# A two-stage attention and gated-mixing kernel: two more operand sets built on chip, the weights prepared in other gaps, and a re-ordered last row

## The chip, the cores and the metric

The kernel runs on one core of a Trainium2 chip. The metric is the device time of one execution in microseconds (us), lower is better. It was run three times: 956.33, 957.35 and 960.95 us, median 957.35.

## The reference

The input `x` is 4 batches x 1024 tokens x 128 channels, float32. Two residual stages follow each other:

```python
x = x + layernorm(attention(layernorm(x), weight))
x = x + layernorm(mixing(layernorm(x), W_r, W_k, W_v, mu_r, mu_k))

# attention: 16 heads of 8 channels; queries and keys are both y, values are all 128 channels
scores = einsum('bhtk,bhsk->bhts', y, y) / sqrt(8)
o = einsum('bhts,bsc->bhtc', softmax(scores), x)          # x here is the normalised input
out = o (all heads side by side, 16*128 wide) @ weight    # weight: 2048 x 128

# mixing: the token before is mixed in, then a gate and a squared relu
r = sigmoid((mu_r*x + (1-mu_r)*x_prev) @ W_r.T);  k = (mu_k*x + (1-mu_k)*x_prev) @ W_k.T
out = r * (relu(k)**2 @ W_v.T)
```

## The kernel before, in words

**Units of work.** The tokens are cut into 8 rows of 512 (two rows to a batch). A *step* j is one head of one row, so there are 8 x 16 = 128 steps, and each step is two *quads* k = 2j, 2j+1 of 4 blocks of 128 keys: 256 quads in all. The five engines have programs of their own, each an ordered list written by a loop `for k in range(LAST)`, and they meet only at semaphores. An instruction that waits holds back everything behind it on its engine.

**One quad.** `score(k)` on TensorE (line 573, four matmuls of 32 rows) makes 4 x 512 scores in PSUM `ps_s`; `weigh(k)` on ScalarE (line 753) takes their exponential to `e_f`, float32; `cast(k)` (line 424) is a DMA, issued by GpSimd, which writes `e_hi`, the float16 part; `split_quad(k)` on VectorE (line 1103) makes the rest, `e_lo`; `products(k)` on TensorE (lines 592 to 594, twelve matmuls) multiplies both with the split values into `ps_o`. The loop runs `products(k-4)` behind `score(k)` (LAG is 4). Quad 0 has no DMA: VectorE casts it (`round_first`).

**One step.** After its second quad ScalarE takes the result (`take_o`, line 763), VectorE takes its rest (`split_o`, 1109), TensorE multiplies by the head's weights (`project`, 607 to 609, twelve matmuls), VectorE inverts the denominators (`invert`, 1115), ScalarE scales (`scale`, 770) and VectorE adds (`add`, 1122 and 1125). `project(j)` waits until `scale(j-1)` has read `ps_r`; it stands at k = 8 + 2j.

**Score operands.** A score matmul reads `op_s` and `op_t`: for each head the 8 channels in a high part, a low part, and rows with constants and a bound. They are made by transposing the normalised input (`turn_y`, `turn_shift` on TensorE, `take_y`, `take_shift` on ScalarE), writing it to scratch memory in DRAM (`keep_hi`, `keep_lo`, `keep_shift` on the SP queue) and reading it back per head into a ring of four slots (`load_s`, `load_t`, 8 DMAs a step). Since that round trip is long, the operands of the first two steps (`FIRST = 2`, quads 0 to 3) are built on chip: `first_operands` on VectorE (lines 1055 to 1064, 11 instructions) and on TensorE (lines 529 and 538), with ScalarE moving them to the ring. Those of step 2 are loaded by ScalarE's queue (`load_first_t`, 758) and SP, the others by SP (lines 308 and 315).

**Weights.** `weights_less(i)`, i = 0 to 3, subtracts on TensorE a column from four heads' weights (line 552, float32); `weight_base(i)` on VectorE finishes it (1075, 1076); `square_weights`, `weight_sum`, `keep_weight_sum`, `weight_scale` find a scale; `weights_high`, `weights_low` and `weights_neg` make the float16 parts. All must be there before `project(0)`.

**The last row.** After the loop the last step and the second stage of the last row are run in two halves of 256 tokens: `last_take`, `last_split`, `last_project`, `last_invert`, `last_scale`, `last_add`, a norm, a second norm, `last_turn`, `last_zT`, `last_mix`, then `last_key`, `last_gate`, `last_kv` on TensorE, and on VectorE per half `last_gated`, `last_centre`, `last_root`, `last_grow`, each half with its own norm and store. Exponential, square root and tanh need table loads on ScalarE, which the program forces early with a one-element `idle` activation (lines 950, 957, 963).

The loops around the change, in the tensor engine's program:

```python
            first_operands()
            for k in range(LAST):
                if k == LAG - 1:
                    products(0)
                if k == LAG:
                    weights_less(1)
                    weights_less(2)
                    products(1)
                    weights_less(3)
                    weight_sum()
                if k in (LAG + 1, LAG + 2):
                    products(k - LAG + 1)
                if k < QUADS:
                    score(k)
```

Of the kernel before, what the change touches and what calls it, by code (L numbers as in the profile page):

```python
# [30 lines left out]
def sandwich(nc, x, weight, w_r, w_k, w_v, mu_r, mu_k, out):  # L31
# [18 lines left out]
    FIRST = 2  # L50

    ctx = ExitStack()
    with ctx:
# [51 lines left out]

        yf = sb("yf", [P, NB, FIRST * HS], F32)
        sqf = sb("sqf", [P, RB, FIRST * HS], F32)
        n2f = sb("n2f", [P, 2, RB * FIRST], F32)
        comb_s = sb("comb_s", [P, NB, FIRST, 4, HS], F16)
        comb_t = sb("comb_t", [P, RB, FIRST, 4, HS], F16)  # L110

# [130 lines left out]
        def weights_ps(i):  # L242
            return (ps_r[:], ps_r[:], ps_x[:], ps_r[:])[i]
# [25 lines left out]
        def _(sp):  # L269
# [31 lines left out]
            def load_s(j):  # L301
                slot = j % OP_RING
                ge(sp, scored, 2 * (j - OP_RING + 1))
                if j % (2 * H) == 0:
                    sp.wait_ge(scr_s_in[batch_of(j)], 3 * 16)
                    sp.wait_ge(scr_const, 16 * B)
# [3 lines left out]
            def load_t(j):  # L310
                slot = j % OP_RING
                if j % (2 * H) == 0:
                    sp.wait_ge(scr_t_in[batch_of(j)], 4 * 16)
# [6 lines left out]
            sp.wait_ge(scr_const, 16)  # L320
            sp.wait_ge(scr_s_in[0], 3 * 16)
            for j in range(FIRST, OP_RING):
                load_s(j)
            sp.wait_ge(scr_t_in[0], 4 * 16)
            for j in range(FIRST + 1, OP_RING):
                load_t(j)
            for k in range(LAST):
# [17 lines left out]
                if k % 2 == 0 and k // 2 + OP_RING < STEPS:  # L345
# [14 lines left out]
        def _(pool):  # L360
# [21 lines left out]
            nc.gpsimd.memset(comb_s[:, :, :, 3, :], 1.0 / HS).then_inc(comb_const, 1)  # L382
# [92 lines left out]
        def _(pe):  # L475
# [41 lines left out]
            def weight_sum():  # L517
                pe.wait_ge(w_squared, 1)
                pe.wait_ge(w_based, 3)
                nc.tensor.matmul(ps_x[:, 0:1], ones[:], w_sum[:, 0:1], start=True, stop=True).then_inc(w_total, 1)  # L520

            def first_operands():
                pe.wait_ge(comb_s_ok, 1)
                pe.wait_ge(comb_const, 1)
                for h in range(FIRST):
                    for g in range(4):
                        for q in range(2):
                            at = h * 2 * P + q * P
                            mm = nc.tensor.transpose(f16(ps_o[32 * g:32 * g + 32, 0, :])[:, at:at + P],
                                                     comb_s[:, 2 * g + q, h].rearrange("p i k -> p (i k)"), ident16[:])  # L530
                mm.then_inc(first_s, 1)
                pe.wait_ge(comb_t_ok, 1)
                for h in range(FIRST):
                    for i in range(RB):
                        for g in range(4):
                            here = slice(32 * g, 32 * g + 32)
                            dst = f16(ps_o[here, 1, :] if h == 0 else ps_r[here, :])
# [855 lines left out]
```

## Time and profile before

| | |
|---|---|
| runs | 956.33, 957.35, 960.95 us; median 957.35 |
| the profiled execution | 956.48 us, of which the span of its trace is 954.7 us (1.8 us lie around it) |
| TensorE matmul busy | 909.0 us, 95% of the span |
| VectorE / ScalarE / GpSimd busy | 851.3 (89%) / 753.1 (79%) / 329.8 us (35%) |
| mean granted clock of TensorE | 0.986 of full |
| chain that ended last | PE 79%, DVE 5%, POOL 5%, DMA 4% |

TensorE is busy nearly everywhere: of 40 slices only the first two and the last two are under nine tenths. Busy time of matmuls overlaps, so the distance between two starts is the better price of one. The engines are named PE (TensorE; PEld its weight loads), DVE (VectorE), ACT (ScalarE), POOL (GpSimd) and SP in the rows.

### The profile page before, as it was taken

Reading aid. Unit: us, or ns where it says so; the run is one execution under the profiler, and the core shown is the slowest. Engines: PE = TensorE matmul, PEld = TensorE weight load, DVE = VectorE, ACT = ScalarE, POOL = GpSimd, SP = SyncE. Lnnn points to the kernel's source line nnn. Section 1 sums busy time; section 2 is a strip of 40 time slices with the busy share of each in tenths; the row PEclk is TensorE's granted clock in tenths of the full one; section 3 lists DMA queues with packets and bytes.
Section 4 is the critical chain, followed back from the end, with each engine's and each line's share of the span. In section 5 each row is a group of like instructions: output and inputs, shape, how many; then the busy total and the mean of one; then the engine's idle time right before and its main releaser. Section 6 shows DMA issues by size and latency. Waiting matters only on the chain.

```text
span 954.7 us, 17710 instructions
## 1 busy us (share of the span) xinstructions
PE 909.0 (95%) x5979; PEld 439.7 (46%) x5979; DVE 851.3 (89%) x1111; ACT 753.1 (79%) x1047; POOL 329.8 (35%) x484
## 2 busy tenths in 40 slices
PE   4799999999999999999999999999999999999982
PEld 2244444444444444444444444545444444544442
DVE  6789899898899989998988989999889899988976
ACT  5777788888879778888778777888877887788854
POOL 2111413532134634525126262443114451162310
PEclk9999999999999999999999999999999999999995
DMA  5899999999999888999988988899988989889820
GB/s 162 180 213 200 199 199 210 207 202 207 181 182 187 177 179 174 210 193 214 184 180 175 198 167 174 178 220 206 198 178 179 193 180 189 175 174 197 175 56 23
DMA packets 99465, 173.50 MB, mean 182 GB/s; under 512 B 21296, under 2 KB 62128, under 8 KB 99376
## 3 DMA queue, kind: packets, MB, share of 16 engines
q0 software_dynamic: 36720, 133.71, 72.7%
q1 hardware_dynamic: 62464, 38.54, 14.6%
q8 instruction: 48, 0.79, 0.3%
q14 instruction: 41, 0.34, 0.1%
q10 hardware_dynamic: 192, 0.13, 0.1%
HBM read 28.12 MB, written 10.49 MB: 40 GB/s over the span
## 4 chain that ended last, share of the span: by engine, by line
PE 79%; DVE 5%; POOL 5%; DMA 4%; issue 4%; ACT 2%; ACTq 0%; DVEq 0%; POOLq 0%
PE ps_o L592 22%; PE ps_o L594 19%; PE ps_o L593 19%; PE ps_s L573 7%; DMA e_hi<-e_f 4%; PE ps_r L607 3%; PE ps_r L609 3%; PE ps_r L608 3%; DVE e_lo L1103 1%; ACT e_f L753 1%; POOL e_hi L424 1%; POOL fnw L396 1%; POOL nw L394 1%; PE ps_x L634 1%; PE ps_x L630 1%
## 5 line engine op out<-in xcount | busy, mean ns | idle before, releaser
L1103 DVE TENSOR_TENSOR e_lo<-e_f,e_hi 128x2048 f16<-128x2048 f32 x256 | 585.0, 2286 | 64.7 <-DMA e_hi<-e_f 64.3
L753 ACT ACTIVATE e_f<-ps_s 128x2048 f32<-128x2048 f32 x256 | 481.6, 1881 | 135.4 <-PE ps_s L573 128.5
L592 PE MATMUL ps_o<-e_hi,y_hi 128*128 128x512 f16 x1024 | 391.9, 383 | 5.4 <-DVE o_neg L1109 4.8
L594 PE MATMUL ps_o<-e_hi,y_lo 128*128 128x512 f16 x1024 | 389.3, 380 | 0.0
L593 PE MATMUL ps_o<-e_lo,y_hi 128*128 128x512 f16 x1024 | 389.3, 380 | 0.0
L424 POOL DMA_DIRECT2D e_hi<-e_f x255 | 141.5, 555 | 563.0 <-ACT e_f L753 473.6
L592 PEld LDWEIGHTS ps_o<-e_hi,y_hi 128*128 128x128 f16 x1024 | 99.8, 97 | 156.1 <-issue 56.9
L770 ACT ACTIVATE part<-ps_r,rden 128x128 f32<-128x128 f32 x508 | 144.7, 372 | 33.7 <-DVE rden L1115 33.4
L594 PEld LDWEIGHTS ps_o<-e_hi,y_lo 128*128 128x128 f16 x1024 | 100.4, 98 | 121.9 <-issue 1.6
L593 PEld LDWEIGHTS ps_o<-e_lo,y_hi 128*128 128x128 f16 x1024 | 100.5, 98 | 92.2 <-issue 1.8
L573 PE MATMUL ps_s<-op_t,op_s 32*128 32x512 f16 x1024 | 102.5, 388 | 7.0 <-ACT e_f L753 5.6
L607 PE MATMUL ps_r<-w_hi,o_hi 128*128 128x128 f16 x508 | 91.8, 219 | 0.0
L608 PE MATMUL ps_r<-w_lo,o_hi 128*128 128x128 f16 x508 | 91.8, 219 | 0.0
L609 PE MATMUL ps_r<-w_neg,o_neg 128*128 128x128 f16 x508 | 91.7, 219 | 0.0
L1125 DVE TENSOR_TENSOR acc<-acc,part 128x512 f32<-128x512 f32 x119 | 82.9, 697 | 9.0 <-ACT part L770 8.5
L1109 DVE SCALAR_TENSOR_TENSOR o_neg<-o_hi,ps_o 128x512 f16<-128x512 f16 x127 | 85.7, 675 | 0.8 <-ACT o_hi L763 0.8
L763 ACT ACTIVATE o_hi<-ps_o 128x512 f16<-128x512 f32 x127 | 76.2, 600 | 1.3 <-PE ps_o L594 1.3
L573 PEld LDWEIGHTS ps_s<-op_t,op_s 32*128 32x128 f16 x1024 | 26.4, 91 | 69.5 <-issue 50.9
L608 PEld LDWEIGHTS ps_r<-w_lo,o_hi 128*128 128x128 f16 x508 | 49.8, 98 | 15.0 <-issue 0.3
L607 PEld LDWEIGHTS ps_r<-w_hi,o_hi 128*128 128x128 f16 x508 | 49.8, 98 | 15.0 <-issue 0.3
L609 PEld LDWEIGHTS ps_r<-w_neg,o_neg 128*128 128x128 f16 x508 | 49.8, 98 | 0.0
L1115 DVE RECIPROCAL rden<-ps_r 128x4 f32<-128x4 f32 x127 | 22.1, 174 | 5.3 <-PE ps_r L609 4.9
(223 smaller groups left out, 501.2 us busy)
## 6 DMA issues: line engine op xcount, KB each, us to landing
e_hi<-e_f POOLq DMA_DIRECT2D x255, 512.0 KB, 4.9
op_t<-scr_t SPq DMA_DIRECT2D x500, 32.0 KB, 3.6
op_s<-scr_s SPq DMA_DIRECT2D x504, 16.0 KB, 3.5
scr_s<-yT SPq DMA_DIRECT2D x12, 256.0 KB, 4.8
scr_t<-yT SPq DMA_DIRECT2D x12, 256.0 KB, 5.3
out_dram<-res SPq DMA_DIRECT2D x7, 256.0 KB, 5.5
xs<-in_L_attn_x_dram SPq DMA_DIRECT2D x3, 512.0 KB, 6.5
scr_s<-eighth SPq DMA_DIRECT2D x4, 256.0 KB, 5.3
```

The costliest lines, as they stand in the source:

```text
L424: nc.gpsimd.dma_start(flat(e_hi[:, ring]), flat(e_f[:, k % EF_RING])).then_inc(cast_in[ring], 16)
L573: mm = nc.tensor.matmul(ps_s[:, g, :], op_s[here, slot, q * P:(q + 1) * P], op_t[here, slot, :], start=True, stop=True)
L592: nc.tensor.matmul(dst, y_hi[:, b % 2, s, :], e_hi[:, ring, g, :], start=(q == 0 and g == 0), stop=False)
L593: nc.tensor.matmul(dst, y_hi[:, b % 2, s, :], e_lo[:, ring, g, :], start=False, stop=False)
L594: mm = nc.tensor.matmul(dst, y_lo[:, b % 2, s, :], e_hi[:, ring, g, :], start=False, stop=(q == 1 and g == 3))
L607: nc.tensor.matmul(dst, o_hi[:, j % 2, here], w_hi[:, j % H, :], start=True, stop=False)
L608: nc.tensor.matmul(dst, o_hi[:, j % 2, here], w_lo[:, j % H, :], start=False, stop=False)
L609: mm = nc.tensor.matmul(dst, o_neg[:, j % 2, here], w_neg[:, j % H, :], start=False, stop=True)
L753: nc.scalar.activation(e_f[:, k % EF_RING], ps_s[:], ACT.Exp, scale=1.0 / ROOT).then_inc(weighed, 1)
L770: ins = nc.scalar.activation(part[:, j % 2, i, :], ps_r[:, i * P:(i + 1) * P], ACT.Identity, scale=rden[:, j % 2, i:i + 1])
L1103: dve.tensor_tensor(flat(e_lo[:, ring]), flat(e_f[:, k % EF_RING]), flat(e_hi[:, ring]), ALU.subtract).then_inc(split, 1)
L1109: dve.scalar_tensor_tensor(out=o_neg[:, j % 2, :], in0=o_hi[:, j % 2, :], scalar=2.0 ** O_BITS, in1=ps_o[:, j % 2, :], op0=ALU.mult, op1=A ...
```

## The change

It has four parts.

1. `FIRST` goes from 2 to 4: the operands of steps 0 to 3 (quads 0 to 7) are built on chip, in two sets of two steps (`SET = 2`). The second set is a second call of `first_operands` in the middle of the opening. The DMA loads of steps 2 and 3, `load_first_t` among them, go; the first loads are those of steps 4 and 5, step 6 follows at k = 4.
2. The products and the weights of the opening are re-ordered: `products(k-4)` now stands behind `score(k)` from the start, `weights_less` uses other PSUM banks and stands at k = 3 and 4, `weight_sum` at k = 6, `weights_high` at 7, `weights_neg` at 8, `weights_low` at 8. `project(0)` moves from k = 8 to k = 9, with `invert(0)`, `scale(0)` and `add(0)` one later too (`step_at`).
3. In the last row the square root's table load stands behind `last_scale` in place of ahead of it.
4. `last_gate(1)` stands ahead of `last_kv(0)`, and both halves share one last norm: one square root, one `last_root`, one `last_grow` over four blocks.

The diff, cut to its core:

```diff
-    FIRST = 2
+    FIRST = 4
+    SET = 2
         def weights_ps(i):
-            return (ps_r[:], ps_r[:], ps_x[:], ps_r[:])[i]
+            return (ps_o[:, 1, :], ps_o[:, 1, :], ps_r[:], ps_x[:])[i]
+        def step_at(k, lead):
+            if k == lead + 1:
+                return 0
+            return (k - lead) // 2 if k > lead and (k - lead) % 2 == 0 else None
...
# sync
-            for j in range(FIRST, OP_RING):
+            for j in (FIRST, FIRST + 1):
                 load_s(j)
-            for j in range(FIRST + 1, OP_RING):
+            for j in (FIRST, FIRST + 1):
                 load_t(j)
-                if k % 2 == 0 and k // 2 + OP_RING < STEPS:
+                if k % 2 == 0 and FIRST + 2 <= k // 2 + OP_RING < STEPS:
...
# tensor
-            def first_operands():
+            def first_operands(n):
+                pe.wait_ge(comb_s_ok, n + 1)
+                if n == 1:
+                    pe.wait_ge(first_t_in, 2)
...
+                pe.wait_ge(comb_t_ok, n + 1)
+                if n == 1:
+                    pe.wait_ge(yT_ready, 2)
             def weights_less(i):
                 if i == 0:
-                    pe.wait_ge(first_t_in, 2)
+                    pe.wait_ge(shift_ready, 1)
                 if i == 2:
-                    pe.wait_ge(yT_ready, 2)
+                    pe.wait_ge(first_s_in, 2)
                 if i == 3:
-                    pe.wait_ge(w_based, 2)
+                    pe.wait_ge(first_t_in, 3)
...
+                if k == LAG - 1:
                     weights_less(0)
+                    first_operands(1)
+                    weights_less(1)
+                if k == LAG:
+                    weights_less(2)
+                    weights_less(3)
-                if 4 <= k - LAG < QUADS:
+                if 0 <= k - LAG < QUADS:
                     products(k - LAG)
+                if k == LAG + 2:
+                    weight_sum()
-                j = (k - LAG - 4) // 2
-                if (k - LAG - 4) % 2 == 0 and 0 <= j < LAST_STEP:
+                j = step_at(k, LAG + 4)
+                if j is not None and j < LAST_STEP:
                     project(j)
             last_key(1)
+            last_gate(1)
             last_kv(0)
-            last_gate(1)
             last_kv(1)
# scalar
-                if k == 4:
-                    keep_weight_sum()
                 if k == 1:
                     take_y(0, 1)
+                if k == 2:
                     take_shift(0)
                 if k == 3:
-                    load_first_t()
+                    take_first_s(1)
+                    take_second_t()
+                if k == 4:
                     square_weights()
-                if k == 5:
-                    weights_high()
+                if k == 6:
+                    keep_weight_sum()
                 if k == 7:
+                    weights_high()
+                if k == 8:
                     weights_neg()
...
-            nc.scalar.activation(idle[:], consts[:, 0:1], ACT.Sqrt)
             for u in range(HALVES):
                 last_scale(u)
+            nc.scalar.activation(idle[:], consts[:, 0:1], ACT.Sqrt)
...
-            for u in range(HALVES):
-                last_sqrt(2, pair(u), u + 1)
+            last_sqrt(2, slice(0, RB), HALVES)
# vector
                 if k == 2:
+                    first_operands(1)
                     weight_base(0)
-                if k == 3:
                     weight_base(1)
-                    weight_base(2)
-                if k == 4:
-                    weight_base(3)
-                if k == 5:
+                if k in (3, 4):
+                    weight_base(k - 1)
+                if k == 6:
                     weight_scale()
-                if k == 6:
+                if k == 8:
                     weights_low()
...
                 last_centre(1, 2, pair(u), gated, u + 1)
-                last_root(2, pair(u), u + 1)
-                last_grow(1, 2, pair(u), xn, l_x1, u + 1)
+            last_root(2, ALL, HALVES)
+            last_grow(1, 2, ALL, xn, l_x1, HALVES)
```

What that does to the order of the instructions, at three places. First TensorE in the opening, from the third score (quad 2) on. In the names, `ps_o<-ident16,shx` is `turn_shift`, `<-w_raw,less` is `weights_less`, `e_hi`/`e_lo` with `y_hi`/`y_lo` are the products. Before:

```order
L573 MATMUL ps_s<-op_t,op_s 128x512 x4
L514 MATMUL ps_o<-ident16,shx 128x128 x8
L552 MATMUL ps_r<-w_raw,less 128x512
L592 MATMUL ps_o<-e_hi,y_hi 128x512
L593 MATMUL ps_o<-e_lo,y_hi 128x512
L594 MATMUL ps_o<-e_hi,y_lo 128x512
...
L573 MATMUL ps_s<-op_t,op_s 128x512 x4
L552 MATMUL ps_r<-w_raw,less 128x512
L552 MATMUL ps_x<-w_raw,less 128x512
```

And with the change (`comb_s_1` and `comb_t_1` are the second set):

```order
L590 MATMUL ps_s<-op_t,op_s 128x512 x4
L522 MATMUL ps_o<-ident16,shx 128x128 x8
L590 MATMUL ps_s<-op_t,op_s 128x512 x4
L569 MATMUL ps_o<-w_raw,less 128x512
L541 MATMUL ps_r<-ident16,comb_s_1 32x128 x16
L554 MATMUL ps_x<-ident16,comb_t_1 32x128 x32
L569 MATMUL ps_o<-w_raw,less 128x512
L590 MATMUL ps_s<-op_t,op_s 128x512 x4
L569 MATMUL ps_r<-w_raw,less 128x512
L569 MATMUL ps_x<-w_raw,less 128x512
L609 MATMUL ps_o<-e_hi,y_hi 128x512
```

Score 3 is now ahead of all products, and score 4 behind the second set; the first products come behind it and all four `weights_less`.

Second ScalarE at the start of the last row: the last `scale`, the table load, the scaling of the last step. Before:

```order
L904 ACTIVATE o_hi<-ps_o 128x512
L770 ACTIVATE part<-ps_r,rden 128x128 x4
L950 ACT_TABLE_LOAD
L950 ACTIVATE idle<-consts 128x1
L911 ACTIVATE part<-ps_s,rden 128x128 x4
```

With the change:

```order
L923 ACTIVATE o_hi<-ps_o 128x512
L780 ACTIVATE part<-ps_r,rden 128x128 x4
L930 ACTIVATE part<-ps_s,rden 128x128 x4
L971 ACT_TABLE_LOAD
L971 ACTIVATE idle<-consts 128x1
```

The table load is now behind the four `part<-ps_s` activations.

Third VectorE at the very end. Before, this sequence stands there twice, for `ps_x` and for `ps_o`:

```order
L1339 SCALAR_TENSOR_TENSOR gated<-gate,ps_o 128x256
L1287 BN_STATS l_st<-gated 128x6 x2
L1292 BN_AGGR l_mv<-l_st 128x2 x2
L1298 TENSOR_TENSOR l_mid<-gated,l_mv 128x256
L1304 TENSOR_SCALAR l_w<-l_mv,consts 128x2
L1306 RECIPROCAL l_w<-l_w 128x2
L1307 SCALAR_TENSOR_TENSOR l_w<-l_w 128x2
L1308 TENSOR_TENSOR l_w<-l_w 128x2
L1309 SCALAR_TENSOR_TENSOR l_w<-l_w 128x2
L1314 SCALAR_TENSOR_TENSOR xn<-l_mid,l_w,yn 128x128 x2
```

With the change, behind the first half's four rows:

```order
L1356 SCALAR_TENSOR_TENSOR gated<-gate,ps_o 128x256
L1304 BN_STATS l_st<-gated 128x6 x2
L1309 BN_AGGR l_mv<-l_st 128x2 x2
L1315 TENSOR_TENSOR l_mid<-gated,l_mv 128x256
L1321 TENSOR_SCALAR l_w<-l_mv,consts 128x4
L1323 RECIPROCAL l_w<-l_w 128x4
L1324 SCALAR_TENSOR_TENSOR l_w<-l_w 128x4
L1325 TENSOR_TENSOR l_w<-l_w 128x4
L1326 SCALAR_TENSOR_TENSOR l_w<-l_w 128x4
L1331 SCALAR_TENSOR_TENSOR xn<-l_mid,l_w,yn 128x128 x4
```

The first half's five `l_w` rows and its two `xn` rows are gone from ahead of the second `gated`; one set of four-wide rows is left.

## Rows read from the trace of the kernel before

**Rows 1.** Windows: length, busy PE, PEld, DVE, ACT, POOL, granted clock, DMA share, GB/s.

```profile
39.40:44.40 5.00, 0.41 (x8) 0.10 (x4) 4.37 (x2) 4.99 (x5) 0.53 (x1) 0.96 0.94 187
44.40:50.80 6.40, 6.11 (x20) 2.31 (x21) 5.76 (x5) 4.00 (x3) 1.06 (x2) 0.50 1.05 214
...
61.00:926.00 865.00, 859.63 (x5679) 414.92 (x5679) 788.57 (x947) 699.09 (x974) 315.21 (x442) 1.00 0.91 187
926.00:954.70 28.70, 7.78 (x50) 6.16 (x48) 18.38 (x80) 14.68 (x35) 3.20 (x10) 0.65 0.06 19
```

**Rows 2.** The chain that ended last, in the opening: start, us, what.

```profile
28.70 4.23 DMA op_t<-scr_t
...
35.59 4.35 DMA e_hi<-e_f
```

**Rows 3.** The timeline of TensorE: start, us, engine, line, operation, tiles.

```profile
11.80 0.65 PE L538 MATMUL ps_r<-ident,comb_t 128*32 128x128 f16 x16
...
20.21 2.02 PE L552 MATMUL ps_r<-w_raw,less 128*128 128x512 f32 x2
...
26.75 1.02 PE L552 MATMUL ps_x<-w_raw,less 128*128 128x512 f32 x2
...
57.32 0.22 PE L607 MATMUL ps_r<-w_hi,o_hi 128*128 128x128 f16 x1
...
58.09 0.39 PE L573 MATMUL ps_s<-op_t,op_s 32*128 32x512 f16 x4
...
61.11 0.39 PE L573 MATMUL ps_s<-op_t,op_s 32*128 32x512 f16 x4
```

**Rows 4.** The timeline of VectorE in the opening, idle time before in brackets.

```profile
8.78 0.28 DVE L1055 TENSOR_TENSOR yf<-xs,mv 128x128 f32<-128x128 f32 x1
...
11.15 0.20 DVE L1064 TENSOR_SCALAR comb_t<-n2f 128x64 f16<-128x64 f32 x1
...
19.24 2.29 DVE L1103 TENSOR_TENSOR e_lo<-e_f,e_hi 128x2048 f16<-128x2048 f32 x1
...
25.86 2.29 DVE L1103 TENSOR_TENSOR e_lo<-e_f,e_hi 128x2048 f16<-128x2048 f32 x1 [2.72 <-DMA e_hi<-e_f]
```

**Rows 5.** The timeline of ScalarE in the opening.

```profile
20.45 1.02 ACT L748 ACTIVATE shT<-ps_o 128x1024 f16<-128x1024 f16 x1 [0.99 <-PE ps_o L514]
21.37 1.87 ACT L753 ACTIVATE e_f<-ps_s 128x2048 f32<-128x2048 f32 x1
...
53.59 1.14 ACT L770 ACTIVATE part<-ps_r,rden 128x128 f32<-128x128 f32 x4
```

**Rows 6.** The timeline of ScalarE and VectorE in the last row.

```profile
928.41 1.28 ACT L950 ACT_TABLE_LOAD   x1
...
929.81 1.13 ACT L911 ACTIVATE part<-ps_s,rden 128x128 f32<-128x128 f32 x4
...
930.46 0.42 DVE L1273 TENSOR_TENSOR acc<-acc,part 128x256 f32<-128x256 f32 x1 [1.26 <-ACT part L911]
...
933.09 0.30 ACT L920 ACTIVATE l_w<-l_mv,ws 128x4 f32<-128x4 f32 x1 [2.15 <-DVE l_mv L1292]
...
946.06 1.28 ACT L963 ACT_TABLE_LOAD   x1
```

**Rows 7.** The chain that ended last, TensorE's piece for the second gate.

```profile
945.10 0.53 PE ps_o L703 x4
```

**Rows 8.** The timeline of VectorE in the norms of the last row.

```profile
934.75 1.14 DVE L1314 SCALAR_TENSOR_TENSOR yn<-l_mid,l_w,xs 128x128 f32<-128x128 f32 x4
...
945.14 0.42 DVE L1339 SCALAR_TENSOR_TENSOR gated<-gate,ps_x 128x256 f32<-128x256 f32 x1 [1.68 <-PE ps_x L717]
...
946.74 0.22 DVE L1304 TENSOR_SCALAR l_w<-l_mv,consts 128x2 f32<-128x2 f32 x1
...
950.76 0.22 DVE L1304 TENSOR_SCALAR l_w<-l_mv,consts 128x2 f32<-128x2 f32 x1
...
951.80 0.62 DVE L1314 SCALAR_TENSOR_TENSOR xn<-l_mid,l_w,yn 128x128 f32<-128x128 f32 x2
```

More of the change, by code:

```diff
@@ L104, in sandwich @@
         diag = sb("diag", [P, H], F32)
[L106 to L110, printed above, removed]
+        yf = [sb(f"yf_{n}", [P, NB, SET * HS], F32) for n in range(FIRST // SET)]
+        sqf = [sb(f"sqf_{n}", [P, RB, SET * HS], F32) for n in range(FIRST // SET)]
+        n2f = [sb(f"n2f_{n}", [P, 2, RB * SET], F32) for n in range(FIRST // SET)]
+        comb_s = [sb(f"comb_s_{n}", [P, NB, SET, 4, HS], F16) for n in range(FIRST // SET)]
+        comb_t = [sb(f"comb_t_{n}", [P, RB, SET, 4, HS], F16) for n in range(FIRST // SET)]
         op_s = sb("op_s", [P, OP_RING, 2 * P], F16)
@@ L381, in _ @@
             nc.gpsimd.memset(less[:, P - 1:P], 0.0).then_inc(const_ok, 1)
-            nc.gpsimd.memset(comb_s[:, :, :, 3, :], 1.0 / HS).then_inc(comb_const, 1)
+            for n in range(FIRST // SET):
+                nc.gpsimd.memset(comb_s[n][:, :, :, 3, :], 1.0 / HS).then_inc(comb_const, 1)
             def inv_root(part_, s, before, v, y, a, var, n, eps=consts[:, 0:1], bias=None, mean=None):
@@ L636, in row_part @@
                     mm.then_inc(kv_ps, 1)
-            first_operands()
+            first_operands(0)
             for k in range(LAST):
-                if k == LAG - 1:
-                    products(0)
-                if k == LAG:
-                    weights_less(1)
-                    weights_less(2)
-                    products(1)
-                    weights_less(3)
-                    weight_sum()
-                if k in (LAG + 1, LAG + 2):
-                    products(k - LAG + 1)
                 if k < QUADS:
@@ L753, in weigh @@
                 nc.scalar.activation(e_f[:, k % EF_RING], ps_s[:], ACT.Exp, scale=1.0 / ROOT).then_inc(weighed, 1)
-            def load_first_t():
-                act.wait_ge(scr_t_in[0], 4 * 16)
-                for g in range(4):
-                    nc.scalar.dma_start(*op_t_load(FIRST, g)).then_inc(op_in[FIRST], 16)
             def take_o(j):
@@ L833, in keep_weight_sum @@
                 act.wait_ge(w_total, 1)
-                nc.scalar.activation(w_sum[:, 1:2], ps_x[:, 0:1], ACT.Copy).then_inc(w_summed, 1)
+                nc.scalar.activation(w_sum[:, 1:2], ps_r[:, 0:1], ACT.Copy).then_inc(w_summed, 1)
             def normalize_half():
@@ L851, in take_first_t, with take_second_t @@
                 nc.scalar.activation(op_t[:, j, :], src, ACT.Copy).then_inc(first_t_in, 1)
+            def take_second_t():
+                act.wait_ge(first_t, 3)
+                nc.scalar.activation(op_t[:, SET:FIRST, :].rearrange("p j t -> p (j t)"), f16(ps_x[:]),
+                                     ACT.Copy).then_inc(first_t_in, 1)
             def turn_in_ffn_weights():
@@ L858, in _ @@
             normalize_half()
-            take_first_s()
+            take_first_s(0)
             take_first_t(0)
@@ L884, in _ @@
                     take_o(j)
-                j = (k - LAG - 5) // 2
-                if (k - LAG - 5) % 2 == 0 and 0 <= j < LAST_STEP - 1:
+                j = step_at(k, LAG + 5)
+                if j is not None and j < LAST_STEP - 1:
                     scale(j)
@@ L1212, in _ @@
                     split_o(j)
-                j = (k - LAG - 5) // 2
-                if (k - LAG - 5) % 2 == 0 and 0 <= j < LAST_STEP:
+                j = step_at(k, LAG + 5)
+                if j is not None and j < LAST_STEP:
                     invert(j)
-                j = (k - LAG - 6) // 2
-                if (k - LAG - 6) % 2 == 0 and 0 <= j < LAST_STEP - 1:
+                j = step_at(k, LAG + 6)
+                if j is not None and j < LAST_STEP - 1:
                     add(j)
```

74 lines of the change are left out of this document (39 added, 35 removed).

## The prediction

> **What bounds the kernel now.** I read the windows view first, to find the stretches where TensorE isn't the bound. From 61 to 926 us it is busy for 859.63 of 865.00 us at full granted clock [rows 1]: whatever reaches that stretch earlier ends earlier by as much. What the change touches lies outside it. From 39.4 to 44.4 us TensorE works 0.41 us of 5.00, and in the next 6.4 us its granted clock is 0.50, the lower of its two levels (1.2 GHz), so that 6.11 us of work took about twice what it needs: some 4.6 us of idling and 3.1 us of slowness, 7.7 us in all [rows 1]. Next I read the chain of waits, which says why. Score 4 waited for a load of operands that landed at 28.70 + 4.23 = 32.93 us; then a cast DMA took 4.35 us from 35.59 [rows 2]; and products 4 wait for `split_o(0)`, which stands behind `weights_low` on VectorE. The timelines give the prices. Two scores one quad apart start at 58.09 and 61.11, so a quad costs TensorE 3.02 us, and the projection between 57.32 and 58.09 costs 0.77 [rows 3]. Score 12, at 61.11, is my mark: from k = 12 on both programs have the same order.
>
> **The opening, walked with the new order.** VectorE ends the first `e_lo` at about 19.24 + 2.2 = 21.45 [rows 4]. There the second operand set now stands: the same 11 instructions ran for the first set from 8.78 to 11.35, 2.6 us, so it is done at 24.0, and the next `e_lo`, behind two `weight_base`, comes later than its 25.86. That start was itself the end of a 2.72 us wait for a DMA [rows 4], so part of the delay is covered, and products 1 need it only after 33.
>
> ScalarE idled 0.99 us ahead of `shT` at 20.45 [rows 5]. With `weigh(2)` moved ahead of it that idling is filled: the exponential (1.87) runs from 19.4 to 21.3, `shT` (1.02) to 22.2, and `weigh(3)`, whose score no longer stands behind products 0, to 24.1.
>
> TensorE does score 3 at 21.5, then waits for `shT`, which frees the bank of `weights_less(0)`: 22.4. That one took 2.02 us where the array was slow, against 1.02 for a later one [rows 3]; I take 1.9, to 24.3. The second set is 48 small transposes; 16 of them took 0.65 [rows 3], so 1.95, to 26.2. Then ScalarE's copy of 1024 columns, as long as the 1.02 of `shT` [rows 5], ends near 27.3, while `weights_less(1)` runs beside it to 27.9. **Score 4 starts at about 28.0, not 33.0.** The load for which it waited is gone, and this is where the gain comes from.
>
> From there to score 12 TensorE has eight quads (24.2), `weights_less` 2 and 3 (1.0 each), two projections (1.5) and `weight_sum`. The last has no shown row of its own: below a `weights_less` (1.0), above nothing; I take 0.5, it is a one-column product. Sum 28.2: score 12 would start at 56.2 if TensorE never waited. It will wait. `project(1)` stands one quad behind `project(0)`, and needs `scale(0)`, which stands on ScalarE behind `weigh(10)` and `take_o(2)`. Score 10 ends at 28.0 + 18.1 + 2.0 + 0.5 + 0.8 + 0.3 = 49.7; then 1.87, some 0.6 for `take_o` (an estimate: half the columns of `shT`, 1.02), 1.14 [rows 5] and some tenths of hand-over give 53.5, where TensorE, with products 6 done, is there at 52.4: 1.1 us. `weights_high` and `weights_neg`, each as long as an exponential, stand ahead of `weigh(8)` and `weigh(9)`, and hold scores 9 and 10 up by about half a microsecond each. So 2.1 us of waits: **score 12 at 58.3, gain 2.8 us.** The idle gaps are each near 1 us, and I count on none like the 5 us one that preceded the slow stretch [rows 1].
>
> What hides the rest: the casts are issued well ahead (the second exponential to the fourth end at 19 to 24, their `e_lo` run from 29 to 37), so a landing time of 4.35 [rows 2] is covered, for the fourth to sixth cast by a microsecond or less. The operand DMAs of steps 2 and 3 are gone from SP and ScalarE; those of step 4 are wanted at about 43 and of step 5 at about 50, ahead of which SP has 15 us and more. `weights_low` is again ahead of `split_o(1)` but no longer ahead of `split_o(0)`. The bounds of this term: nothing waits, 61.11 - 56.2 = 4.9; and waits as long as the ones removed short of half a microsecond, 0.5.
>
> **Start of the last row.** The table load runs from 928.41 for 1.28 us and `last_scale` starts at 929.81; behind it VectorE's `last_add` starts at 930.46 after 1.26 us of idling [rows 6]. With the load behind, `last_scale` can start at 928.41, 1.40 earlier; VectorE has 1.26 to win, the rest is its own work. The load then runs beside the two `last_add` halves, until about 931.2, and the square root, which began at 933.09 [rows 6], is then wanted at 933.09 - 1.26 = 931.8: covered by 0.6. **Gain 1.26.** The Trainium skill ("ScalarE: Activation LUTs", section "What ACT_TABLE_LOAD costs") puts a switch at about 2.66 us, the load plus a drain of 1.38; by that the gain would be 1.4 higher. Here the trace disagrees: no second part of that size lies between the load's end at 929.69 and 929.81, so I keep 1.26.
>
> **The last norm.** `last_kv(0)` moves behind `last_gate(1)`, whose piece of the chain is 0.53 [rows 7], so VectorE's first `gated` goes from 945.14 to 945.67. A half costs VectorE 946.74 - 945.14 = 1.60 up to its root, the root 951.80 - 950.76 = 1.04, and growing four blocks 1.14 [rows 8]. So 945.67 + 3.20 + 1.04 + 1.14 = 951.05, against 951.80 + 0.62 = 952.42 before. **Gain 1.37.** The square root's load begins after the second tanh in both versions (946.06 before [rows 6]) and with the one-element activation is over by 947.6, a microsecond ahead of its use at 948.6; before, the first half waited for it. The first store leaves 1 us later and the two lie closer together; the last one still sets the end.
>
> **The sum** is 2.8 + 1.26 + 1.37 = 5.4 us. Against the profiled execution's own 956.48 that is 951.1; the median of the runs, 957.35, lies 0.9 above that execution, and I put the forecast between: **951.4 us**.
>
> **The rivals.** A measurement of this kernel can tell about 0.5%, 4.8 us, from no change, and the forecast is only just beyond.
> - *The wait moves.* ScalarE and VectorE now hold seven pieces of weight work and a whole operand set in the stretch where TensorE is meant to be fed. If each of casts 4 to 6 or its `e_lo` comes a microsecond late, the opening gives 0.5 to 1.5 us: total gain 3.1 to 4.1, 953 to 954. For it: VectorE's 2.6 us, the casts' thin cover. Against: TensorE has queued work of its own from 24 to 33. Chance 0.18.
> - *The array slows down again.* If waits pile up around projections 0 and 1 as they did around 39.4 to 44.4, the 3.1 us of slow work come back [rows 1]: gain 2.3, 954.9. Chance 0.08.
> - *Nothing waits.* The opening gives up to 4.9: 949.2. Chance 0.07.
> - *Slower.* TensorE now starts its dense work at 28 and not at 22, after a stretch of small transposes with gaps. If the array stays on its lower level through the quads that follow, each one costs 3 us more. The first eats the opening's 2.8, the second the rest of the 5.4, from the fourth on the kernel is slower by more than can be overlooked (4 x 3.0 - 5.4 = 6.6), and with all six ahead of `project(0)` it ends at 956.8 + 12.6, near 969. Against it: before, about 4 us after 18.7 with less to do than now, the array was fast. The Trainium skill ("TensorE: Matmul & The Clock Gate", section "HAM oscillation") warns of this pattern, gaps that put a warm array back to its slow level; the trace agrees, in the stretch at granted clock 0.50 behind the one with 0.41 us of work. Chance 0.05.
> - *The change doesn't do what it says* in the tail, if the square root's load lands on the path: at most the 1.3 us of each part. It lies inside the first rival's range.
>
> **How the numbers follow.** The forecast (0.62) spans opening gains of 1.9 to 3.8, total gains of 4.5 to 6.4, so about 950 to 952.5; some 0.06 of it falls within 0.5%. Faster by over 0.5%: 0.56 + 0.07 = 0.63. Within 0.5%: 0.06 + 0.18 + 0.08 = 0.32. Slower: 0.05. The range runs from 949.0, nothing waits, to 955.0, the slowed array.
>
> **What would show it.** Score 4 within a microsecond of 28 and score 12 at 57 to 59.5; no window of granted clock 0.50 between 30 and 61; no idling of `last_add` behind the table load; four `xn` blocks in one run, and the stretch from the end of the dense part to the end of the span, 28.7 us from 926.00 [rows 1], shorter by 2.6; and a dense part that ends some 3 us earlier than before. I am wrong if score 12 isn't earlier than 60, or if TensorE's quads between 28 and 40 are spaced 5 us.

## The result, and the profile after

The changed kernel takes 949.02 us (median of 4 runs, 946.98 to 951.60), the kernel before 957.13 us beside it: ratio 0.9914, 95% interval 0.9889 to 0.9939. Forecast were 951.4, a gain of 5.4 against the profiled execution; measured are 8.1 us between the medians. The direction and the places are right, the size was too small, and the time stands at the very end of the range. Of all runs below one, of 974.71 us at a granted clock of 0.941 (kept_busy), was slower as a whole and is left out of its ratio.

The profiled execution of the changed kernel has a span of 945.2 us, 9.5 less than before. Divided at two marks (score 12, and the last inverse ahead of the last row's halves, 927.03 before and 919.76 after):

| stretch | before | after | gain | predicted |
|---|---|---|---|---|
| to score 12 | 61.11 | 56.24 | 4.87 | 2.8 |
| dense stretch | 865.92 | 863.52 | 2.40 | 0 |
| last row to the end | 27.67 | 25.44 | 2.23 | 2.6 |

TensorE's timeline of the changed kernel in the opening (answers to [rows 3]; `weights_less(0)`, the second set's second part, scores 4 and 8, projection 1, score 12):

```profile
22.18 2.05 PE L569 MATMUL ps_o<-w_raw,less 128*128 128x512 f32 x2 [0.39 <-ACT shT L763]
...
24.56 1.08 PE L554 MATMUL ps_x<-ident,comb_t 128*32 128x128 f16 x32
...
27.11 0.40 PE L590 MATMUL ps_s<-op_t,op_s 32*128 32x512 f16 x4
...
41.12 0.40 PE L590 MATMUL ps_s<-op_t,op_s 32*128 32x512 f16 x4
...
52.46 0.22 PE L624 MATMUL ps_r<-w_hi,o_hi 128*128 128x128 f16 x1 [0.89 <-ACT part L780]
...
56.24 0.39 PE L590 MATMUL ps_s<-op_t,op_s 32*128 32x512 f16 x4
```

Score 4 is at 27.11 and not at 32.97, and the one longer wait left is the predicted one, of projection 1 for `scale(0)`: 0.89. The windows view shows that the idle and the slow stretch of [rows 1] are gone; TensorE is busy all of the 16 us from 24 on, and its granted clock is 1.00 throughout:

```profile
24.00:40.00 16.00, 16.00 (x117) 7.29 (x117) 13.29 (x21) 10.95 (x10) 2.11 (x4) 1.00 0.93 201
40.00:46.00 6.00, 5.89 (x33) 2.27 (x32) 6.00 (x4) 6.00 (x5) 1.06 (x2) 1.00 0.82 165
46.00:56.20 10.20, 9.08 (x63) 4.24 (x61) 9.70 (x9) 8.26 (x14) 1.41 (x3) 1.00 1.05 237
```

The timeline of the last row (answers to [rows 6] and [rows 8]; `last_add`, the load, the second gate, the first product, the first `gated`, the joint growing):

```profile
921.95 0.43 DVE L1290 TENSOR_TENSOR acc<-acc,part 128x256 f32<-128x256 f32 x1
...
922.60 1.28 ACT L971 ACT_TABLE_LOAD   x1
...
935.53 1.06 PE L718 MATMUL ps_o<-wT,mix 128*128 128x128 f32 x4
...
936.39 1.06 PE L732 MATMUL ps_x<-wT,kr 128*128 128x128 f32 x4
...
937.49 0.42 DVE L1356 SCALAR_TENSOR_TENSOR gated<-gate,ps_x 128x256 f32<-128x256 f32 x1 [2.53 <-PE ps_x L732]
...
941.74 1.14 DVE L1331 SCALAR_TENSOR_TENSOR xn<-l_mid,l_w,yn 128x128 f32<-128x128 f32 x4
```

`last_add` no longer idles: it comes 2.19 us behind the last inverse and not 3.43. The joint norm ends at 942.88, 5.39 us behind the first `gated`, before 7.28.

### The profile page after: what moved, and what is told of

The parts are those of the page before. It is cut to its first block, busy times and chain, and to the rows that moved or that the text cites. A ratio compares the mean times of both kernels' runs of the same rounds, so it can differ in the third digit from the quotient of the medians.

```text
span 945.2 us, 17798 instructions
## 1 busy us (share of the span) xinstructions
PE 907.9 (96%) x6027; PEld 440.4 (47%) x6027; DVE 850.9 (90%) x1117; ACT 753.9 (80%) x1048; POOL 311.2 (33%) x485
## 4 chain that ended last, share of the span: by engine, by line
PE 81%; DVE 6%; POOL 4%; issue 3%; DMA 3%; ACT 3%; DVEq 0%; POOLq 0%; ACTq 0%
PE ps_o L609 22%; PE ps_o L611 20%; PE ps_o L610 20%; PE ps_s L590 7%; DMA e_hi<-e_f 3%; PE ps_r L624 3%; PE ps_r L626 3%; PE ps_r L625 3%; DVE e_lo L1121 2%; ACT e_f L768 2%; PE ps_x L651 1%; PE ps_x L647 1%; POOL e_hi L432 1%; POOL fnw L408 1%; PE ps_x L641 1%
```

## The experiments

Sixteen runs followed, of ten further kernels and of repeats. Of each trace I read the starts of all 256 scores, since whatever holds TensorE up between two scores makes them stand further apart. In the table: the starts of scores 4, 8 and 12, the time of quads 12 to 60, the time from score 60 to the last inverse, and from there to the end of the span (read to 0.1 us, so the last column is good to 0.05).

```
                  score 4  score 8  score 12  quads 12-60  60-last inverse   last row
before              32.97    44.49     61.11       163.64           702.28      27.67
before_again        33.37    44.89     61.12       163.84           703.47      27.97
before_third        32.96    44.47     60.53       163.63           702.98      27.96
tail_alone          33.13    44.64     59.84       163.67           702.89      24.60
kept_busy           32.64    44.16     58.06       168.41           701.02      27.31
kept_busy_again     32.97    44.49     58.43       168.60           700.59      27.38
set_by_dma          33.42    49.33     64.44       163.63           704.12      24.91
extra_loads         27.47    46.80     63.40       164.85           699.97      25.38
opening_alone       26.76    40.78     55.90       164.16           699.94      28.00
changed             27.11    41.12     56.24       163.64           699.88      25.44
after_again         27.03    41.04     56.16       163.64           699.35      25.45
after_more          27.45    41.47     56.58       163.64           699.90      25.38
load_ahead          27.04    41.05     56.16       163.87           700.02      26.15
kv_first            27.41    41.43     56.55       163.63           701.71      24.51
kv_first_again      26.76    40.78     55.90       164.50           703.11      24.49
scale_early         27.69    41.85     55.91       164.23           702.10      25.16
two_norms           27.67    41.69     56.80       164.16           704.01      26.23
both_edits          27.74    41.76     55.82       164.35           701.20      24.53
```

**The changed kernel again** (after_again, no edit).

> The changed kernel once more. Its first trace is 9.5 us shorter than that of before: 4.9 us are there at score 12, 2.4 us come in the dense stretch between score 12 and the last projection, 2.2 us in the last row. Theory A (the dense stretch differs by chance of the execution): score 12 again at 56.2 within 0.2, the last row again 25.7 within 0.2, but the dense stretch anywhere between 863 and 868 us, so that the time over several runs is 948 to 951. Theory B (the change makes the dense stretch faster): it is again 863.3 within 0.5, and so in every trace that has the changed opening.

Median 948.59 (5 runs), ratio 0.9909 (0.9877 to 0.9941). Score 12 at 56.16, the last row 25.45, the dense stretch 862.99: as theory B has it. But theory B asks the same of every trace with the changed opening, and kv_first below has that opening with dense stretches of 865.34 and 867.61. Neither theory is right as it stands; more on it below.

**The last row alone** (tail_alone): parts 3 and 4 of the change on the kernel before.

```diff
# the kernel before
-            nc.scalar.activation(idle[:], consts[:, 0:1], ACT.Sqrt)
             for u in range(HALVES):
                 last_scale(u)
+            nc.scalar.activation(idle[:], consts[:, 0:1], ACT.Sqrt)
...
+            last_gate(1)
             last_kv(0)
-            last_gate(1)
...
-                last_root(2, pair(u), u + 1)
-                last_grow(1, 2, pair(u), xn, l_x1, u + 1)
+            last_root(2, ALL, HALVES)
+            last_grow(1, 2, ALL, xn, l_x1, HALVES)
```

> The kernel before with the three edits of the last row alone (table load behind the scales, second gate ahead of the first product, one joint last norm). Expected by theory A: the opening as before (score 12 at 61.1), the last row 25.7 in place of 27.9 us, so 2.2 us faster, about 955. By theory B the dense stretch stays at 865.7. A rival for the last row: its gain in the changed kernel came from arriving in another state of the array's clock, then it is under 1.5 us here.

Median 953.72 (10 runs) against 956.01, ratio 0.9970 (0.9955 to 0.9985): 2.3 us faster. In the trace the last row took 24.60, even 0.8 less than in the changed kernel: there the second gate's matmuls took 0.69 and the first product's 0.61, where the changed kernel shows 1.06 and 1.06. The array rose to its faster level during the second gate here, some 16 us behind the last inverse, and in the changed kernel only during the second product, some 18 us behind it.

**The opening alone** (opening_alone): the changed kernel with the whole last row as before.

> The changed kernel with the whole last row as before (table load ahead, first product ahead of the second gate, two norms). Score 12 again at 56.2 to 56.8 and the last row as long as before, 27.7 from the last inverse on; so 4.9 us of the gain stay, and the median is 951 to 952. If the parts add up, this gain and the 2.3 us of the kernel with the new last row alone make the whole, 7.5 to 8 us. If the opening's gain were partly given back in the dense stretch, it would be 3 us or less.

Median 952.18 against 956.98, ratio 0.9946 (0.9928 to 0.9964): 4.8 us faster. With the 2.3 of the last row that makes 7.1 of the 8.1. The opening's gain isn't given back. (This trace lost 2.0 us at quads 92 to 108, where the changed kernel's lost 0.2 to 0.3; see the dense stretch.)

**The new order without the second set** (set_by_dma): the changed kernel, but steps 2 and 3 come by DMA as before (the waits and loads that follow from it are not shown).

```diff
# the changed kernel
-    FIRST = 4
+    FIRST = 2
...
-                    first_operands(1)
                     weights_less(1)
...
-                    take_first_s(1)
-                    take_second_t()
+                    load_first_t()
```

> The changed kernel with its new order of products and weights, but the operands of steps 2 and 3 loaded by DMA as before. If the loads' wait was what held the opening: score 4 not before 31 to 33, and score 12 at 59.5 to 61, 3 to 5 us later than in the changed kernel; time 952 to 954. If the new order of products and weights was what brought the gain: score 12 within 1 us of 56.2, time about 950.

Median 956.32 against 956.01: ratio 1.0007 (0.9984 to 1.0030): no gain in all, where 952 to 954 were expected. The last row kept its gain (24.91), so the opening lost as much as that gave. The trace shows it. Its score 4:

```profile
33.42 0.61 PE L589 MATMUL ps_s<-op_t,op_s 32*128 32x512 f16 x4 [6.01 <-DMA op_t<-scr_t]
```

Score 4 waits 6.01 us for the load, as late as before, and score 12 comes at 64.44, 3.3 us later than before and 8.2 later than in the changed kernel, since the products that once filled this wait now stand behind score 4. So the re-ordering (part 2) by itself is a loss; it pays only with the operands on chip. I had expected 3 to 5 us more than in the changed kernel and not 8.2.

**The loads issued all the same** (extra_loads): the second set stays on chip, but SP also issues the 16 loads of steps 2 and 3, into a buffer that nobody reads.

```diff
# the changed kernel, sync
+            for j in (2, 3):
+                for g in range(4):
+                    sp.dma_start(ex_s[32 * g:32 * g + 32, j - 2, :], op_s_load(j, g)[1]).then_inc(ex_in, 16)
...
             for j in (FIRST, FIRST + 1):
                 load_s(j)
```

> The changed kernel with the 16 loads of steps 2 and 3 issued by SP all the same, ahead of those of step 4, into a buffer that nobody reads. Nothing waits for them but SP's queue. Theory S (SP's queue is the second bound of the first batch): in the changed kernel each step's last load is issued some 11 to 12 us ahead of its score, in the kernel that was only kept busy 4 to 7 us ahead, and the latter lost 3.7 us in quads 44 to 60 and showed no gain over ten runs. With 16 issues of 0.6 us more the lead falls to about 3 us: score 8 or 10 waits, or quads 12 to 60 take 1 to 4 us more than 27.19, 26.86, 26.86, 27.31, 27.64 and 27.75 us for eight; median 951 to 953. If the lead of SP does not matter, the median is within 1 us of 949.

Median 956.48 against 956.98, ratio 0.9992 (0.9980 to 1.0003), and the changed kernel in the same job took 948.07: 16 DMAs that nobody waits for cost 8.4 us, more than the 2 to 4 that were expected. Of these 7.2 are there at score 12. Score 4 is at 27.47, as in the changed kernel; then score 8 waits for the loads of step 4. Score 8, and the windows around it:

```profile
46.80 0.61 PE L603 MATMUL ps_s<-op_t,op_s 32*128 32x512 f16 x4 [5.24 <-DMA op_t<-scr_t]
```

```profile
39.00:46.00 7.00, 2.56 (x12) 0.97 (x10) 6.79 (x11) 3.87 (x3) 0.53 (x1) 0.88 0.91 181
46.00:58.00 12.00, 11.20 (x58) 4.70 (x59) 6.72 (x5) 7.96 (x6) 1.06 (x2) 0.78 0.64 146
```

TensorE works 2.56 us of 7.00, and then the slow level is back, with a granted clock of 0.78 over 12 us. It is again a wait with a slow stretch behind it, as in the kernel before. The timeline of SP shows what the loads of step 4 waited for: 32 issues in a row without a gap, from 24.36 to 47.31, 0.72 us each; the last of step 4 starts at 45.03, against 33.90 in the changed kernel:

```profile
24.36 6.83 SPq L337 DMA_DIRECT2D ex_s<-scr_s  x8
31.23 6.02 SPq L341 DMA_DIRECT2D ex_t<-scr_t  x8
37.37 5.32 SPq L321 DMA_DIRECT2D op_s<-scr_s  x8
42.73 4.58 SPq L328 DMA_DIRECT2D op_t<-scr_t  x8
```

Whether an issue is long by itself or because transfers ahead of it are not done, these rows don't tell. Nor is this the order of the kernel before, whose ScalarE issued four of the 16 and whose SP took step 4 ahead of step 5; there the last load of step 4 landed at 40.49.

**TensorE kept busy** (kept_busy, kept_busy_again): the kernel before with 8 unused products behind score 6 and 8 behind score 7.

```diff
# the kernel before, tensor
+                if k in (6, 7):
+                    for _ in range((8, 8)[k - 6]):
+                        nc.tensor.matmul(ps_x[:], y_hi[:, 0, 0, :], y_hi[:, 0, 0:4, :].rearrange("p k c -> p (k c)"),
+                                         start=True, stop=True)
```

> The kernel before with 16 extra products of 512 columns, 8 behind score 6 and 8 behind score 7, where TensorE waits; their result is written to a free bank and not used. If the slow stretch from 44.4 to 50.8 us is an outcome of the idling ahead of it, no window of granted clock 0.50 is left there, products 4 and projection 0 take 3.4 us and not 6.1, and score 12 comes 2 to 3 us earlier, at 58 to 59. If the array slows down for another reason, score 12 stays at 61.

> A second trace of the kernel before with TensorE kept busy behind scores 6 and 7. Its first lost 3.7 us between quads 44 and 60, one wait of 2.0 us for an operand load among them, and ten runs showed no gain of the 3.05 us won at score 12. Theory S (SP's queue issues loads too late for an earlier TensorE): quads 12 to 60 again cost over 2 us more than 163.6. If it was chance, they cost 163.6 here.

The slow stretch is an outcome of the idling: with the extra work the granted clock stays at 1.00 and score 12 comes at 58.06 and 58.43, 2.1 to 3.1 us earlier than in the three traces of before.

```profile
39.40:44.40 5.00, 3.99 (x24) 1.42 (x21) 4.71 (x3) 4.98 (x5) 0.62 (x2) 1.00 0.95 185
44.40:50.80 6.40, 5.99 (x42) 2.94 (x39) 6.40 (x6) 5.70 (x6) 0.96 (x2) 1.00 1.07 209
```

(The Trainium skill, "TensorE: Matmul & The Clock Gate", section "HAM oscillation", has idle gaps as what puts the array back to its slow level; these rows agree, 1.00 here against 0.96 and 0.50 in [rows 1].) Yet the median over ten runs is 956.33 against 956.01, ratio 0.9991 (0.9972 to 1.0009): nothing gained. All of it is lost again in quads 12 to 60, 168.41 and 168.60 us where every other kernel takes 163.6 to 164.9. Of these 4.8 to 5.0 us, 2.9 in the first trace and 2.4 in the second are scores that wait for operand loads (0.35, 0.59 and 1.97; 0.54 and 1.85). The longest wait has the slow level behind it: from 115.00 to 118.50 of the second trace the granted clock is 0.61, and the quad that starts at 115.02 takes 1.69 us more than in the other traces. The longest wait of the second trace:

```profile
115.02 0.40 PE L573 MATMUL ps_s<-op_t,op_s 32*128 32x512 f16 x4 [1.85 <-DMA op_t<-scr_t]
```

An earlier TensorE alone runs into SP's queue. From the last issue of a step's loads to its first score it is 10.4 to 12.9 us at steps 7 to 11 of the kernel before and 10.7 to 13.2 in the changed one, but 4.2 to 6.9 in these two traces, and a load there lands up to 6.0 us behind its issue.

**The pieces of the last row** (load_ahead, two_norms, kv_first): the changed kernel with one of them as before.

> The changed kernel with the square root's table load ahead of the last scales again. Theory: the last row is longer by the 1.24 us that the load held VectorE up, 26.9. If a switch of tables cost 2.66 us in all, it would be longer by 2.6.

> The changed kernel with the two separate last norms of before; second gate ahead of the first product and load as changed. The prediction priced the joint norm at 1.37 with 0.53 lost to the moved gate, so alone it is worth 1.9: the last row gets 1.9 longer, 27.6. VectorE's extra work is one root, 1.04, and the first half's wait for the square root's load was 0.88 before; if that wait no longer occurs, only 1.0 is lost, 26.7.

> The changed kernel with the first product ahead of the second gate again, as it was before; load, joint norm and opening as changed. In the changed kernel the first gated row of the last half starts at 937.49 behind that product, and the second gate ahead of it took 0.85 us. VectorE has 3.2 us of work from there to the joint root, so theory: the whole end comes 0.8 us earlier, the last row 24.9 in place of 25.7. Rival: VectorE then waits for the second gate's tanh or the second product between the halves, and the end is the same within 0.2.

load_ahead: `last_add` idles 1.25 us again and comes 3.42 us behind the last inverse in place of 2.19, so the load costs 1.23, and not the 2.6 of the other theory. Since the array then reaches its faster level in time for the product (0.61 in place of 1.06), 0.5 comes back, and the last row is 0.7 longer. two_norms: 0.8 longer, a little less than the lower of the two expected values (1.0): the second root, without the first half's old wait for the load. kv_first: the first `gated` comes 16.81 us behind the last inverse in place of 17.73, and the last row is 0.94 shorter in two traces. So `last_gate(1)` ahead of `last_kv(0)` is a step backwards. The medians, 949.53, 950.80 and 948.29 in one job, with ratios to the kernel before of 0.9913, 0.9917 and 0.9893 and intervals of 0.2 to 0.3% to each side, can't rank differences of this size.

**`scale(0)` one quad earlier** (scale_early), and with kv_first's edit (both_edits).

```diff
# the changed kernel, scalar; in vector the same for invert
-                j = step_at(k, LAG + 5)
-                if j is not None and j < LAST_STEP - 1:
+                j = (k - LAG - 5) // 2
+                if (k - LAG - 5) % 2 == 0 and 0 <= j < LAST_STEP - 1:
                     scale(j)
```

> The changed kernel with invert(0) and scale(0) at k = 9, one quad earlier, behind project(0) itself. In the changed kernel project(1) waits 0.89 us for scale(0), behind weigh(10) and take_o(2) on ScalarE. Theory: that wait goes and score 12 starts at 55.4, 0.9 earlier. Rival: VectorE now waits for project(0) ahead of e_lo 7, and weigh(10) starts later, so that the wait moves to score 11 or products 7 and score 12 stays within 0.3 of 56.2.

> The changed kernel with both edits that helped in a trace: first product ahead of the second gate (last row 0.94 us shorter), invert(0) and scale(0) one quad earlier (opening 0.91 us shorter). Together 1.8 us faster than the changed kernel: median about 947, if the dense stretch gives nothing of it back; 948.5 if it does.

> The changed kernel beside it, on the same chip: median 948.5 to 949.5; score 12 at 56.2 to 56.8, the dense stretch between 863 and 868 us by chance of the execution.

From score 4 to score 12 it is 28.22 us (scale_early) and 28.08 (both_edits) in place of 29.13: the 0.9 is there, and the rival fails. In scale_early score 4 itself came 0.6 us later than in the changed kernel, so its score 12 stands at 55.91; its median is 949.07 (4 runs, ratio 0.9897, 0.9876 to 0.9919), no gain over the changed kernel that could be told from noise. both_edits also has the shorter last row, 24.53. Its median is 947.98 against 948.07 of the changed kernel beside it (4 runs each; ratios 0.9903 and 0.9908): no difference. Its dense stretch took 2.0 us more, 865.55 against 863.54.

**Whose is the dense stretch?** (before_again, before_third, kv_first_again)

> The kernel before, a second trace. Over the 14 traces so far the dense stretch differs at few places; quads 92 to 108 cost the three traces of the changed kernel 0.2 to 0.3 us over the shortest and the kernel before 1.9. If that is an effect of the changed opening, it is 1.9 again here within 0.3. If it is chance of each execution, it may be anything from 0 to 4.

> The same, a third trace: the same expectations. Score 12 at 61.1 and the last row at 27.7 in either case.

> Its program is that of the changed kernel up to the last row, yet quads 92 to 108 cost 2.67 us over the shortest in its first trace, against 0.2 to 0.3 in the three of the changed kernel. If the loss belongs to the build, it is 2.67 again within 0.3; if it is chance, it need not be.

In 16 of the 30 stretches of eight quads from score 12 on, all these traces (kept_busy aside) agree within 0.1 us; the differences sit in the others, above all at quads 92 to 108 and 148 to 164. Quads 92 to 108 take at least 56.88 us. Three traces of the changed kernel lie 0.34, 0.28 and 0.18 above that; the kernel before 1.93, 2.19 and 3.86; kv_first, whose program up to there is the changed kernel's, 2.67 and 2.55. Most of it lies between scores 94 and 95: 4.64 us in each trace of the changed kernel, 6.59 and 6.47 in kv_first, 5.84, 6.11 and 7.78 in the kernel before. So it is not the opening (kv_first has the same).

The traces show where it comes from, on GpSimd. Between the casts of these quads it works on the norm of the next batch, and one small instruction of that, a power of 8 elements per partition, takes 1.68 or 3.61 us. It stands in the queue ahead of a cast, and that DMA's issue waits for it. First the changed kernel, then kv_first, with the `e_lo` and the product that come late:

```profile
326.37 1.68 POOL L402 TENSOR_TENSOR nw<-nw,consts 128x8 f32<-128x8 f32 x1
```

```profile
327.10 3.61 POOL L402 TENSOR_TENSOR nw<-nw,consts 128x8 f32<-128x8 f32 x1
335.61 2.29 DVE L1121 TENSOR_TENSOR e_lo<-e_f,e_hi 128x2048 f16<-128x2048 f32 x1 [1.51 <-DMA e_hi<-e_f]
338.64 0.38 PE L609 MATMUL ps_o<-e_hi,y_hi 128*128 128x512 f16 x1 [0.75 <-DVE o_neg L1127]
```

This divides all eighteen traces: in the five where the instruction takes 1.67 or 1.68 us (changed, after_again, after_more, load_ahead, extra_loads) scores 94 and 95 are 4.64 apart, and in the thirteen where it takes 3.61 they are 5.84 to 8.60 apart. Each kernel with more than one trace always has the same of the two durations, so it goes with the build; opening_alone, two_norms, scale_early and both_edits have the long one. Why the same instruction is longer in one build, no run here tells; it stays open. The same instruction stands again at quads 148 to 164: those take 56.55 to 57.36 us in the three traces where it takes 1.68 (load_ahead, opening_alone, scale_early), and 57.68 to 60.54 in the others, where it takes 3.6 to 3.8. But there the traces of one kernel differ besides, by 1.2 us for the changed kernel and by 1.6 for the kernel before, and that is chance of the execution.

## Why the prediction was right or wrong

**Where the missing time was.** The traces differ by 9.5 us where 5.4 were forecast. Two terms make the difference: the opening gave 4.87 and not 2.8, and the dense stretch, which the sum has at nothing, gave 2.40. The last row gave 0.4 less than forecast.

**What bounds the kernel: right.** Score 12 was a good mark. The gain of the opening reached the end; the median of opening_alone shows it.

**Score 4 at 28.0: nearly right**, 27.11. VectorE's set was done at 23.9 (24.0), `weights_less(0)` took 2.05 (1.9). The array was faster from the second set on: 32 small transposes took 1.08 and not 1.3. (The level of the array in the first 23 us is to be read from durations: the windows view has a granted clock of 1.00 there, though products of 512 columns start 0.43 us apart until 23.3 in the kernel before and 0.22 apart behind it.)

**From score 4 to score 12: the first step that failed.** I had 30.3 us, 28.2 of work and 2.1 of waits; it took 29.13, 27.6 of work and 1.5 of waits. `weights_less` 2 and 3 took 1.82 and not 2.0, and `weight_sum` made its quad 0.12 longer and not 0.5. Of the waits, projection 1's was 0.89 (predicted 1.1); those of scores 9 and 10, to which I gave 1.0 behind `weights_high` and `weights_neg`, were 0.19 and 0.35 by the spacing of the scores. So the waits were mis-sized by 0.6 us, the work by 0.6 and score 4 by 0.9: together the 2.1 us between 58.3 and 56.24. The waits were the right ones, at the places where they were forecast. That score 12 stands at 56.2, the bound for "nothing waits", is luck: it did wait, but started earlier and had less to do.

**What hid the rest: right in the outcome, thinner than I wrote.** I wrote that the loads of step 4 were wanted at about 43 and had 15 us and more. SP issued from 24.40 on, and score 8 started at 41.12; but the last load of step 4 was issued only at 33.90, behind 11 others, and landed at 35.94, so the margin was 5.2 us. extra_loads shows how fast it goes: with 16 issues more in front of them the same load starts 11 us later, and score 12 comes 7.2 us later. I priced the removed loads only by the wait that they ended on and not by the queue that they stood in. In the kernel before that queue cost nothing beyond the wait of score 4 (the loads of step 4 landed 4.0 us ahead of score 8), so this is not what made the forecast too small; but with TensorE 3.4 us earlier at score 8 and the old queue, that margin would have been 0.6 by my estimate (41.12 - 40.49).

**The slow stretch: right.** It went because the idling went; kept_busy shows it by itself. But there it was no gain in all, since the loads came late behind it.

**The table load: right**, 1.24 (predicted 1.26), and load_ahead puts back 1.23. The Trainium skill ("ScalarE: Activation LUTs", section "What ACT_TABLE_LOAD costs") has about 2.66 us for a switch; the traces disagree, 1.28 us for the load and the next activation 1.29 behind its start (928.41 and 929.70 before).

**The last norm: too good by a third of a microsecond.** VectorE's part was exact, 5.39 us from the first `gated` to the end (predicted 5.38). The moved gate cost 0.86, not the 0.53 of [rows 7]: that piece had run while the array's level rose, and in the changed kernel it stood where the array was still slow. In tail_alone, where the level rose during it, it cost 0.53.

**The dense stretch: the second step that failed.** I wrote that whatever reaches this stretch earlier ends earlier by as much, and so put it at nothing, without a reason why it should take the same time in both kernels. It took 2.40 us less. 1.6 of them lie at quads 92 to 108, where GpSimd's power took 1.68 us and not 3.61, and that goes with the build and not with the new opening, which kv_first has too; 1.0 lies at quads 148 to 164, where traces of one kernel differ by as much. I had no reason to expect this part of the gain: as far as the forecast goes it is luck. Without it the traces differ by 7.1 us, which is also what the medians of opening_alone and tail_alone give together.

**The rivals.** "Nothing waits" came nearest in number, at 949.2 and with 0.07, but not in mechanism: 1.5 us of waits were there. The array didn't slow down again. The wait moved in kept_busy and extra_loads, not in the changed kernel, and there it moved to SP's queue and not to VectorE or the casts.

## What to carry to other kernels

When loads leave a queue or join it, look at what stands behind them in it: here 16 loads that nobody waited for put score 12 back by 7.2 us. A faster engine gains nothing by itself if the queue that feeds it is only just ahead; read for each unit of work the distance from the last issue to its use. And don't take a stretch that a change doesn't touch for constant: compare it unit by unit, in more than one trace, before its difference is counted as gain or loss of the change. And price a piece on TensorE at the level that the array has where the piece will stand, not where it stood.

## What the runs showed of the hardware

- A DMA issue on SP's queue took 0.3 to 1.5 us in the opening of the changed kernel, one 2.35; eight of them per step took some 5.8 to 6.2 us of a step's 6.8 in the kernel before. 16 unused ones of 16 and 32 KB put score 12 back by 7.2 us.
- The array's level depended on what TensorE did before: granted clock 1.00 with 3.99 us of work in 5.00, and 0.50 behind 0.41 us of work in 5.00. Behind a wait of 1.85 us in kept_busy_again it was 0.61 over 3.5 us. In the last row the same four matmuls took 0.61 or 1.06 us, by when they came.
- One GpSimd instruction, a power of 128x8 elements, took 1.68 us in some builds and 3.61 in others, again in each further trace of a build, and what hung on the casts behind it came 1.2 us and more later.
